# An expert layer's first two products as three bf16 matmuls, and a context norm folded into later weights

## The reference, cut to what matters

```
x1 = einsum('bsh,ehf->bsef', x, W1) + b1        # H=128 -> F=256, E=8 experts
x2 = einsum('bsh,ehf->bsef', x, W2) + b2
z = x1 * x2
g = einsum('bsef,efg->bseg', z, Wg) + bg        # the gate
o = g * sigmoid(g) * (einsum('bsef,efg->bseg', z, Wl) + bl)   # the linear
y = einsum('bsef,efh->bseh', o, W3) + b3
return einsum('bse,bseh->bsh', combine, y)      # combine: top 2 of 8

# block 3, last attention
yn = _ln(ctx, a2_lny_g, a2_lny_b)     # (ctx - mean) * rsqrt(var + eps) * g + b
k = einsum('btc,hcd->bhtd', yn, wk);  v = einsum('btc,hcd->bhtd', yn, wv)
```

## Time and profile before

| | |
|---|---|
| median of three runs | 4445.98 us (4444.93 to 4448.55) |
| the profiled execution | 4435.46 us |
| its span | 4433.6 us |
| TensorE busy (matmuls) | 4082.9 us, 92% |
| VectorE | 3436.2 us, 78% |
| ScalarE | 2732.0 us, 62% |
| GpSimd | 2695.9 us, 61% |
| mean granted TensorE clock | 0.941 |

### The profile page before, as it was taken

How to read it: one execution, slowest core, us unless ns; L and a number is a source line. 1 busy time by engine, 2 the same in 40 slices (tenths; PEclk the granted TensorE clock), 3 DMA queues, 4 the chain that set the end, 5 groups by cost and what they waited for, 6 DMA issues and landing times. The chain is left out here.

```text
span 4433.6 us, 102799 instructions
## 1 busy us (share of the span) xinstructions
PE 4082.9 (92%) x40217; PEld 2922.3 (66%) x40217; DVE 3436.2 (78%) x6755; ACT 2732.0 (62%) x5298; POOL 2695.9 (61%) x2421
## 2 busy tenths in 40 slices
PE   7999999889988999999699999995996899999967
PEld 4777777655555777777557777774664577777754
DVE  6999998567778888888688888875554888888842
ACT  5777777534436777777467777771441677777721
POOL 3888788646674777777447777772002476777720
PEclk9999999889998999999699999995997999999975
DMA  4333333113331111111011111100000111111000
GB/s 113 90 94 94 89 95 89 47 62 114 112 98 58 54 37 54 39 52 38 19 44 53 37 54 45 45 30 18 1 1 28 43 46 45 50 49 45 30 12 9
DMA packets 107229, 236.66 MB, mean 53 GB/s; under 512 B 13496, under 2 KB 43464, under 8 KB 105368
## 3 DMA queue, kind: packets, MB, share of 16 engines
q1 hardware_dynamic: 106296, 230.03, 17.7%
q10 hardware_dynamic: 448, 0.06, 0.0%
HBM read 164.87 MB, written 50.26 MB: 49 GB/s over the span
## 5 line engine op out<-in xcount | busy, mean ns | idle before, releaser
L466 POOL TENSOR_TENSOR wst<-wst 125x384 bf16<-125x384 f32 (+1 forms) x1536 | 1632.6, 1063 | 833.0 <-ACT wst L664 768.3
L664 ACT ACTIVATE wst<-ps 125x448 f32<-125x448 f32 x3072 | 1498.5, 543 | 408.1 <-PE ps L164 399.1
L721 DVE TENSOR_TENSOR wst<-wst 125x512 bf16<-125x512 f32 (+1 forms) x1536 | 1404.0, 915 | 269.7 <-ACT wst L664 254.5
L164 PE MATMUL ps<-big,cx 128*125 128x448 bf16 (+1 forms) x6144 | 1435.5, 355 | 0.0
L164 PEld LDWEIGHTS ps<-cx,wst 125*128 125x128 bf16 x23040 | 1105.4, 98 | 354.4 <-issue 60.5
L164 PE MATMUL ps<-cx,wst 125*128 125x65 bf16 (+2 forms) x23040 | 1202.3, 204 | 27.5 <-POOL wst L466 13.3
L164 PEld LDWEIGHTS ps<-big,cx 128*125 128x125 bf16 (+1 forms) x6144 | 814.6, 137 | 287.4 <-issue 23.0
L164 PE MATMUL ps<-cx,big 128*128 128x500 bf16 (+1 forms) x2688 | 713.3, 318 | 27.8 <-DVE wst L691 15.0
L688 DVE CUSTOM_DVE_ANT_0 wst<-ps,wst 128x500 bf16<-128x500 f32 x896 | 603.7, 674 | 162.0 <-PE ps L164 122.8
L613 ACT ACTIVATE wst<-ps 128x500 bf16<-128x500 f32 x896 | 531.1, 593 | 221.9 <-PE ps L164 174.3
L691 DVE TENSOR_REDUCE wst<-ps 128x1 f32<-128x500 f32 x896 | 600.3, 670 | 36.1 <-PE ps L164 26.8
(11 more groups left out here) (203 smaller groups left out, 4232.7 us busy)
## 6 DMA issues: line engine op xcount, KB each, us to landing
cx<-ctxT SPq DMA_DIRECT2D x96, 375.0 KB, 3.5
cx<-ctxN SPq DMA_DIRECT2D x64, 377.9 KB
cx<-in_ctxN SPq DMA_DIRECT2D x64, 375.0 KB
cx<-ctxT SPq DMA_DIRECT2D x96, 187.5 KB, 3.8
ctxN<-cx SPq DMA_DIRECT2D x32, 377.9 KB
ynN<-cx SPq DMA_DIRECT2D x32, 377.9 KB
cx<-ynN SPq DMA_DIRECT2D x32, 377.9 KB
cTs<-in_ctxT SPq DMA_DIRECT2D x64, 187.5 KB, 6.8
```

What stands on the lines that cost most here:

```text
L164: return t.matmul(o, l, r, start=start, stop=stop, skip_group_check=True)
L466: g.tensor_tensor(pl[r][0:KP, at:], pf[r][0:KP, at:], pf[r][0:KP, at:].bitcast(BF16)[:, 1::2], ALU.subtract).then_inc(s["plp"], 1)
L664: e.activation(pf[T % 3][0:KP, cols], bank(2 + n2 % 3, 448)[0:KP], ACT.Exp, scale=scale).then_inc(s["ev"], 1)
L721: v.tensor_tensor(pl[r][0:KP, 0:to], pf[r][0:KP, 0:to], pf[r][0:KP, 0:to].bitcast(BF16)[:, 1::2], ALU.subtract).then_inc(s["pl"], 1)
```

## The change

Expert stage:

- up and mid are no longer f32. Each operand is held as a high and a low bf16 half, and each product becomes three bf16 matmuls (high x high, high x low, low x high) into the same PSUM accumulation. down() stays f32.
- The halves have to be made. For x once (`xh` by ScalarE, `xl` by GpSimd), for each expert's weights once (`wh` by ScalarE, 1536 columns in one instruction; `wl` by GpSimd, 768 columns twice), and for z twice in every step (`zh` by ScalarE, `zl` by GpSimd, 448 columns each).
- Their places in the streams: on ScalarE `zh` comes after the sigmoids and `wh` of the next expert right behind it when n % 4 == 3; on GpSimd `zl` is first in the step, `wl` of the next expert behind it when n % 4 == 3, and the context norm's instructions follow.
- The scale g and bias b of the context norm are gone from this stage (L907 and L909). They move into the weights of the last attention: g multiplies the folded key matrix and the folded value matrix, and b goes through the value and output weights into the constant row `crow` (a bias on the keys shifts all scores of a row alike and drops out of the softmax).
- The context is turned in 6 transposes of 125 x 128 (two 64-column blocks at once), into two banks and not three; the evictions (L1142, L1096 of before) are 128 x 375 twice, where they were 64 x 500 three times. A step takes 11 banks. The transposed context is stored by four DMAs of a quarter where there was one.

`a2`: four more loads, eight more small matmuls before the turn of x, two more small ScalarE copies; `dve_fold` multiplies g in on both parts of the key fold (one of them was a ScalarE copy), and the value fold takes g as a per-partition scale.

```diff
@@ pool_fold / act_fold / dve_fold, f == 4
+            for j in range(0, H // per if f == 4 else 0):
+                w.wait_ge(s["bcast"], 64)
+                w.wait_ge(s["f1"], jobs1[f] + j + 1)
+                v.tensor_tensor(fold_out(n)[:, per * j:per * j + per, :], bank(4 + j).rearrange("p (h c) -> p h c", c=n),
+                                lyg.unsqueeze(1).broadcast_to([128, per, C]), ALU.mult).then_inc(s["f1d"], 1)
...
+                    if f == 4:
+                        w.wait_ge(s["bcast"], 64)
+                        e.activation(o, bank(k)[0:n, :], ACT.Identity, scale=lyc[:, 0:1]).then_inc(s["f2a"], 1)
@@ sp_f0
-                    w.wait_ge(s["ntl"], 3 * b + 3)
-                    y.dma_start(yT2[b], cs[b % 3]).then_inc(s[f"stT_{b % 3}"], 16)
+                    w.wait_ge(s["ntl"], 2 * b + 2)
+                    for r in (0, 64):
+                        of = cs[b % 3][:, M // 2:] if r else cs[b % 3][:, 0:M // 2]
+                        y.dma_start(yT2[b][r:r + 64, 0:M // 2], of[0:64, :]).then_inc(s[f"stT_{b % 3}"], 16)
+                        y.dma_start(yT2[b][r:r + 64, M // 2:], of[64:128, :]).then_inc(s[f"stT_{b % 3}"], 16)
@@ pool_f0
-            w.wait_ge(s["bcast"], 32)
-            for b in range(B + 1):
-                if b < B:
+            for c in range(4):
+                cols = slice(512 * c, 512 * c + 512)
+                w.wait_ge(s["fh"], c + 1)
+                g.tensor_tensor(xl[:, cols], xT[:, cols], xh[:, cols], ALU.subtract).then_inc(s["fl"], 1)
+                w.wait_ge(s["fl"], c + 1)
+
+            def low(e):
+                w.wait_ge(s["fh"], weights_high(e))
+                for i in range(2):
+                    cols = slice(768 * i, 768 * i + 768)
+                    g.tensor_tensor(wl[e % 2][:, cols], ew[e % 2][:, cols], wh[e % 2][:, cols], ALU.subtract).then_inc(s["fl"], 1)
+                    w.wait_ge(s["fl"], weights_low(e) - 1 + i)
+
+            low(0)
+            for n in range(B + 2):
+                if n < NE:
+                    u = n % 2
+                    for f in range(2):
+                        cols = slice(448 * f, 448 * f + 448)
+                        w.wait_ge(s["fh"], z_high(n, f))
+                        if n >= 2:
+                            w.wait_ge(s["gl"], 2 * n - 2)
+                        g.tensor_tensor(zl[u][:, cols], zz[u][:, cols], zh[u][:, cols], ALU.subtract).then_inc(s["fl"], 1)
+                        w.wait_ge(s["fl"], z_low(n, f))
+                    if n % 4 == 3 and n < NE - 1:
+                        low(n // 4 + 1)
...
-                    w.wait_ge(s["n3"], 3 * b + 2)
-                    g.tensor_tensor(v, v, bcx[0][0:KP].unsqueeze(1).broadcast_to([KP, KT, C]), ALU.mult).then_inc(s["n3"], 1)
-                    w.wait_ge(s["n3"], 3 * b + 3)
-                    g.tensor_tensor(v, v, bcx[1][0:KP].unsqueeze(1).broadcast_to([KP, KT, C]), ALU.add).then_inc(s["n4"], 1)
@@ pe_f0
-                    w.wait_ge(s[f"e_{e % 2}"], 32 * (e // 2 + 1))
+                    w.wait_ge(s["fh"], weights_high(e))
+                    w.wait_ge(s["fl"], weights_low(e))
                     for f in range(2):
                         cols = slice(128 * f, 128 * f + 128)
-                        mm(t, bank(take(), 448), ew[e % 2][:, 0:256][:, cols], tok8(xT, c), True, True).then_inc(s["u1"], 1)
-                        mm(t, bank(take(), 448), ew[e % 2][:, 256:512][:, cols], tok8(xT, c), True, True).then_inc(s["u2"], 1)
+                        for at, done in ((0, "u1"), (256, "u2")):
+                            o = bank(take(), 448)
+                            wih, wil = wh[e % 2][:, at:at + 256][:, cols], wl[e % 2][:, at:at + 256][:, cols]
+                            mm(t, o, wih, tok8(xh, c), True, False)
+                            mm(t, o, wih, tok8(xl, c), False, False)
+                            mm(t, o, wil, tok8(xh, c), False, True).then_inc(s[done], 1)
...
                             for i2 in range(2):
-                                w.wait_ge(s["z"], 2 * m + i2 + 1)
-                                r = mm(t, bank(k, 448), wm[:, i2, cols], zz[u][:, 448 * i2:448 * i2 + 448], i2 == 0, i2 == 1)
+                                half = slice(448 * i2, 448 * i2 + 448)
+                                w.wait_ge(s["fh"], z_high(m, i2))
+                                mm(t, o, wmh[:, i2, cols], zh[u][:, half], i2 == 0, False)
+                                w.wait_ge(s["fl"], z_low(m, i2))
+                                mm(t, o, wmh[:, i2, cols], zl[u][:, half], False, False)
+                                r = mm(t, o, wml[:, i2, cols], zh[u][:, half], False, i2 == 1)
...
-                        for i2 in range(4):
-                            r = t.transpose(bank(k)[0:64, KP * i2:KP * i2 + KP], ns[b % 4][:, 4 * g + i2, :], idf[0:KP, 0:KP])
+                        for i2 in range(3):
+                            r = t.transpose(bank(k)[:, KP * i2:KP * i2 + KP], two[:, 3 * g + i2], idf[0:KP, 0:KP])
@@ act_f0
+                if n < NE:
+                    u = n % 2
+                    for f in range(2):
+                        cols = slice(448 * f, 448 * f + 448)
+                        w.wait_ge(s["z"], 2 * n + f + 1)
+                        if n >= 2:
+                            w.wait_ge(s["gl"], 2 * n - 2)
+                        e.activation(zh[u][:, cols], zz[u][:, cols], ACT.Copy).then_inc(s["fh"], 1)
+                    if n % 4 == 3 and n < NE - 1:
+                        high(n // 4 + 1)
@@ sp_a2, pe_a2
+            for v, name in ((lyg, "a2lyg"), (lyc, "a2lyc"), (lyv, "a2vc"), (lyo, "a2oc")):
+                y.dma_start(v, a[name]).then_inc(s["bcast"], 16)
...
+            w.wait_ge(s["bcast"], 64)
+            for m in range(4):
+                r = mm(t, bank(6)[:, m:m + 1], lyv[:, m, :], lyc[:, 1:2], True, True)
+            r.then_inc(s["qbm"], 1)
+            mm(t, bank(7, 128)[0:1], one[0:1, 0:1], row[2], True, False)
+            w.wait_ge(s["cr"], 2)
+            for m in range(4):
+                r = mm(t, bank(7, 128)[0:1], lyr[:, m:m + 1], lyo[:, m, :], False, m == 3)
+            r.then_inc(s["qbm"], 1)
             pe_turn(t, w, xn, s["xn"], 176, 1)
+            w.wait_ge(s["cr"], 3)
```

More of the change, by code:

```diff
@@ L234, in dve_fold @@
             per, copies = 512 // n, 128 // n
-            for j in range(0, H // per, 2):
+            for j in range(0, H // per if f == 4 else 0):
[3 more added lines that the diff above has]
+                                lyg.unsqueeze(1).broadcast_to([128, per, C]), ALU.mult).then_inc(s["f1d"], 1)
+            for j in range(0, 0 if f == 4 else H // per, 2):
                 w.wait_ge(s["f1"], jobs1[f] + j + 1)
@@ L243, in dve_fold @@
                 for r in range(copies if n == 64 else 0):
-                    v.tensor_tensor(wbl[n * r:n * r + n, cols], bank(k)[0:n, :], wbh[0:n, cols],
-                                    ALU.subtract).then_inc(s["f2d"], 1)
+                    if f == 4:
+                        v.scalar_tensor_tensor(out=wbl[n * r:n * r + n, cols], in0=bank(k)[0:n, :], scalar=lyc[:, 0:1],
+                                               in1=wbh[0:n, cols], op0=ALU.mult, op1=ALU.subtract).then_inc(s["f2d"], 1)
+                    else:
+                        v.tensor_tensor(wbl[n * r:n * r + n, cols], bank(k)[0:n, :], wbh[0:n, cols],
+                                        ALU.subtract).then_inc(s["f2d"], 1)
         def act_fold(e, w, f, n):
             per, copies = 512 // n, 128 // n
-            for j in range(0 if f in EARLY else 1, H // per, 1 if f in EARLY else 2):
+            for j in range(0 if f in EARLY else 1, 0 if f == 4 else H // per, 1 if f in EARLY else 2):
                 w.wait_ge(s["f1"], jobs1[f] + j + 1)
@@ L814, in build, with weights_high, weights_low, z_high @@
         NE = 4 * E
+        zh = [big[:, 7424 + 448 * i:7872 + 448 * i].bitcast(BF16) for i in range(2)]
+        zl = [big[:, 8320 + 448 * i:8768 + 448 * i].bitcast(BF16) for i in range(2)]
+        wh = [big[:, 9216 + 768 * i:9984 + 768 * i].bitcast(BF16) for i in range(2)]
+        wl = [big[:, 10752 + 768 * i:11520 + 768 * i].bitcast(BF16) for i in range(2)]
+        xh, xl = w32[:, 0:1024].bitcast(BF16), w32[:, 1024:2048].bitcast(BF16)
+        def weights_high(e):
+            return 5 + 9 * e
+        def weights_low(e):
+            return 6 + 10 * e
+        def z_high(n, f):
+            return 5 + n // 4 + 2 * n + f + 1
+        def z_low(n, f):
+            return 6 + 2 * (n // 4) + 2 * n + f + 1
+        def paired(v):
+            return v.rearrange("p (i h) c -> p h i c", h=2)
         def ffn_releases():
@@ L825, in ffn_releases @@
                 if 2 <= n <= B + 1:
-                    r += [("ntl", 3 * (n - 2) + g + 1) for g in range(3)]
+                    r += [("ntl", 2 * (n - 2) + g + 1) for g in range(2)]
             return r
@@ L980, in pe_f0 @@
                     b = n - 2
[L981 removed]
```

(27 more changed lines are left out.)

66 lines of the change are left out of this document (37 added, 29 removed), and 2 rows, old and new, of the table s.

## The result

The changed kernel takes 4415.72 us (median of 4 runs, 4405.2 to 4420.38), the one before 4446.85 in the same session (4 runs, 4444.93 to 4448.55): ratio 0.9927, 95% interval 0.9911 to 0.9942. It is 31 us faster where 39 were forecast.

The account below looks back on a forecast made before the run. TensorE bound the 12.70 us step before; VectorE's 10.24 would after. The stage gives 39.0 us (378.4 against 416.4, start 1.0 earlier), the fold costs 0.2: 38.8 less, 4396.7 profiled, median 4407, range 4388 to 4430.

Parts of the forecast that it names:

- TensorE 9.3 to 9.4 a step, wait 0.85 in mid: Normal expert step: TensorE's work falls to 9.3 to 9.4 us; it waits about 0.85 at mid's third output.
- VectorE's step 10.24: Normal expert step: VectorE's fixed instruction stream sums to 10.24 us and now sets the step.
- `zl` 1.24: GpSimd, each expert step: each `zl` instruction takes 1.24 us, between 0.93 and 1.47, and fits by under a microsecond.
- its rival's 1.1 of overrun: Expert steps: GpSimd's chain stretches by a quarter, overruns by 1.1 us and sets the step; 4447 us, chance 0.12.
- The boundary, 6.2 = 4.3 wait + 1.9 clock: Seven expert boundaries: up waits for GpSimd's `wl`, losing 4.3 us, and the halved clock costs 1.9; 43.4 in all.
- Filling 24.8, 28 steps 286.7, boundaries 43.4, tail 23.5: Expert stage after the change: filling steps, normal steps, boundaries and GpSimd's last chain, together 378.4 us against 416.4.
- The first L1042 comes 1.0 earlier: Start of the expert stage: VectorE's first step begins 1.0 us sooner, since up is faster at half clock too.
- What costs nothing: First splits of x and weights hide behind the routing (uncovered 10 us); extra stores and `a2` work are hidden too.
- nothing but +0.2 in `a2`: Outside the expert stage: folding scale and bias into `a2` costs 0.2 us, bounds 0 and 1.5.
- No clock loss: Rival, expert boundaries: the gaps do not halve TensorE's clock, saving 13 us more; 4394 us, chance 0.15.
- All hidden: Rival, expert steps: ScalarE's hand-over is shorter, TensorE sets the step at 9.4 us; 4383 us, chance 0.06.
- The clock stays low: Rival, expert steps: TensorE stays at half clock, 18.8 us a step; up to 4407 + 240 us, chance 0.05.

Follow-up runs that it names:

- e10: Changed kernel with two 125x768 multiplications per step put back on GpSimd, where scale and bias stood: 4480.52 us, ratio 1.0080 to the kernel before.
- e4: Changed kernel with 24 extra bf16 products on TensorE ahead of its wait at each expert boundary: 4392.63 us, ratio 0.9914 to the kernel before.
- e1: Changed kernel with the next expert's weights split one step earlier, on ScalarE and GpSimd: 4383.4 us, ratio 0.9877 to the kernel before.
- e3: Changed kernel with the expert products in float32 again, without splits of x, z or weights: 4395.94 us, ratio 0.9899 to the kernel before.
- e0: The changed kernel measured again without any edit: 4410.8 us, ratio 0.9932 to the kernel before.
- e9: Changed kernel with weights split early in pieces, ScalarE's square behind its evictions, and two store transfers for four: 4366.25 us, ratio 0.9817 to the kernel before.
- e11: Second measurement of the changed kernel with weights split early in pieces and ScalarE's square behind its evictions: 4354.94 us, ratio 0.9795 to the kernel before.
- e6: Changed kernel with weights split early in pieces and ScalarE's square behind its evictions, first measurement: 4366.83 us, ratio 0.9846 to the kernel before.
- e8: Changed kernel with weights split one step earlier and GpSimd's subtraction cut to 8 columns from the third expert on: 4366.46 us, ratio 0.9829 to the kernel before.
- e2: Changed kernel with transposes as before, twelve of one 64-column block into three banks, one store: 4407.98 us, ratio 0.9929 to the kernel before.
- e5: Changed kernel with ScalarE's square moved behind its three evictions: 4412.84 us, ratio 0.9942 to the kernel before.

## Why the prediction was right, and where its sizes were off

The range held the result, and the forecast case is the one that came. By its own steps:

*TensorE 9.3 to 9.4 a step, wait 0.85 in mid.* Measured 9.26 and 0.92, at the place named.

*VectorE's step 10.24.* Measured 10.18, its pieces within 0.1. Laying an engine's fixed stream out from rows without the other's waits gave the bound to 1%.

*`zl` 1.24.* Measured 1.08 each, between the bounds. GpSimd did not set the step: its rival's 1.1 of overrun did not come, but e10 shows that 3.6 us more would have brought it.

*The boundary, 6.2 = 4.3 wait + 1.9 clock.* Measured 6.9 = 4.8 + 2.1 (e4). TensorE idled 5.58, forecast 5.4. The wait is longer because the two halves of `wl` took 3.95, not 3.2 (3.36 in e1): L1153 runs between them and holds up the second, which takes 2.23 for the first one's 1.64. Each of the seven gaps was followed by the halved clock anew (ten products 3.84 us behind the first, twelve 4.47 to 4.64 behind the others, in place of 2.44); this is what the Trainium skill, page "TensorE: Matmul & The Clock Gate", section on HAM oscillation, says of a repeated wait.

*Filling 24.8, 28 steps 286.7, boundaries 43.4, tail 23.5.* Measured 25.2, 285.0, 48.5 and 22.5 (1272.00 to 1294.48): 2.8 more together.

*"The first L1042 comes 1.0 earlier" and "What costs nothing": the step that failed.* Counted from the stage's start it comes 3.1 later (57.32 us after the first L144 against 54.20). I had hidden `xh`, `xl` and `wl` behind the routing, as if work on ScalarE and GpSimd took nothing from VectorE beside it. GpSimd's `wl` runs from 887.84, and beside it the first comparison of the routing, on VectorE and on the path, takes 2.70. VectorE, then TensorE:

```profile
889.57 2.70 DVE L868 TENSOR_TENSOR big<-big 128x1024 bf16<-128x1024 f32 x1
892.19 1.21 DVE L869 TENSOR_TENSOR big<-big 128x1024 bf16<-128x1024 f32 x1
```

```profile
898.95 3.58 PE L989 MATMUL ps<-idf,big 128*8 128x128 f32 x16 [9.75 <-DVE big L1098]
903.21 7.19 PE L164 MATMUL ps<-wst,big 8*128 8x128 f32 x32 [0.68 <-ACT big L1187]
910.78 1.67 PE L164 MATMUL ps<-xn,big 128*128 128x448 bf16 x4 [0.38 <-DVE x L1102]
```

Before it took 1.23, TensorE's gap 8.28 and the 32 products 4.63 in place of 7.19. Without the split all three are as before (e3: 1.23, 8.27 and 4.66). The windows of 1 us, before and then after, show the clock in these products:

```profile
904.00:905.00 1.00, 1.00 (x11) 1.00 (x10) 1.00 (x6) 0.00 (x0) 0.00 (x0) 1.00 0.00 0
904.00:905.00 1.00, 1.00 (x6) 1.00 (x6) 0.69 (x3) 0.00 (x0) 0.00 (x0) 0.50 0.00 0
```

All eleven runs with the split have the longer gap (9.7 to 10.9) and 7.2 for the products, the three without it 8.3 and 4.6 to 4.8; that the longer gap is what keeps the half clock is inferred from this. The two add 4.0 us. The 1.0 forecast for up came (2.8 from the products' end to the first L1112, before 3.8). So 4.1 us of the missing 7 are here, 2.8 in the sums above: the stage gave 32.0, not 39.0.

*The stages behind, put at nothing but +0.2 in `a2`.* In e0 `a2` with cross-attention 3 is +0.3 (852.82 against 852.55), as forecast; its extra work is hidden. But cross-attention 1 is 3.4 longer (822.35 against 818.92), `f1` with cross-attention 2 is 2.5 and the stage behind it 1.2. For the first the rows of the profile after show the start. They are SyncE's last store, first load, first and last doubling transfer (L331 and L332 copy the queries from one half of the partitions to the other), and TensorE's first product with them:

```profile
1296.75 0.37 SPq L915 DMA_DIRECT2D ynN<-cx  x1
1308.11 0.34 SPq L427 DMA_DIRECT2D cx<-ctxT  x1
...
1315.29 0.48 SPq L331 DMA_DIRECT2D big<-big  x1
...
1317.12 0.63 SPq L332 DMA_DIRECT2D big<-big  x1
```

```profile
1323.70 0.58 PE L164 MATMUL ps<-diff,big 128*128 128x500 bf16 x1 [12.20 <-DMA big<-big]
```

The last store is issued 2.3 us after L144 (1294.48; before 0.7), the first load 13.6 after it (before 12.0). The doubling starts sooner than before (20.8 after L144 against 22.3), but TensorE gets it 6.6 us after its last issue, where before, e3, e9 and e11 have 0.9 to 2.0. The four stores are so at most 1.6 of it, and e3, which has them too, has 818.61 for the whole of cross-attention 1. The doubling is late in after and e0 and also in e1, e4, e6, e8 and e10 (5.2 to 6.3), but not in e11, which is e6's kernel, so the kernel alone does not decide it. Why it lands late, and what the 2.5 and the 1.2 are, no run tells; e1, e4 and e6 have 0.6 to 0.7 for `f1` with cross-attention 2.

*The end.* The profiled execution of after lost 8 more in the last stage, whose first matrix products ran at half clock (1.86 us for two, before 1.02). e0, the same kernel, did not (191.3 against 191.0 from the first L144 behind cross-attention 3), nor did it lose the 3.4 that after has in `a2` with cross-attention 3 (856.18 against 852.82). So these are scatter between executions. They make up most of the 13 us by which this profile's span is over e0's (4418.6 against 4405.8). The profiled execution of before in turn lies 10.5 under its median, for which I know no cause: profile against profile e0 is 27.8 us faster, by the medians 35. That the whole came out at 31, close to the stage's 32.0 though the stages behind lost 7, is in part luck of this scatter.

*What the prediction did not ask.* It added up whole steps and never priced the three parts of the change one by one. By e3 the bf16 products, from which it took 2.1 us a step on TensorE, cost 15 us in sum, because VectorE's step and the boundaries took back more than that.

*The rivals.* No clock loss: excluded by the rows of 0.50 and by e4. All hidden: the step is VectorE's. The clock stays low: it came back after each boundary.

The rule that I needed is written down. The Trainium skill, page "SBUF — State Buffer", section "Who interferes with whom", says that a VectorE instruction with two SBUF inputs, or in a mode that uses both of its port pairs, and a GpSimd one that reads SBUF exclude each other for a whole instruction, and that a reduction or an instruction with one SBUF input outside such a mode does not. The traces agree row by row: L1148 (1.65 for 0.17), L1153 (2.40 for 0.96) and L868 (2.70 for 1.23) are held, L1146 and L1158 (0.94 to 0.95) and those with an input in PSUM (L1126 0.68) are not, and the held ones go on when GpSimd's instruction has ended. L1148 has one input; that it ran in such a mode no row shows. The prediction had this contention in its rival on GpSimd, and nothing for it in VectorE's stream, where it acted.

## What to carry to other kernels

When work moves to GpSimd, look at what VectorE does in the same microseconds: 3.4 us of subtraction cost VectorE 3.0 us in e1 and 1.8 at a boundary of the changed kernel, and nothing where VectorE read PSUM or reduced. Work that comes once per several steps should be cut up and placed ahead of its use: the same operations cost 48 us in seven boundaries and about 1 us an expert when spread (four steps 40.0 for 47.5, the square moved with it). And run each part of a change alone: of 35 us the transposes and the moved scale and bias gave 50 and the products took 15 back, until their operands were prepared in time.

## What the runs showed of the hardware

GpSimd's 128x768 subtraction held VectorE's 125x12 instruction for 1.65 us in place of 0.17. A float32 transpose of 125x128 took the time of one of 125x64 (0.107 us each), so a pair of blocks costs half. TensorE's clock stayed at 1.00 behind idle times of 1.45 and 2.99 us (e2) and fell behind 3.79 (e1), 5.58 (after) and 6.61 (e5).
